# Attention inside a mixture-of-experts layer: query and key weights merged, value weights behind the attention, mask on VectorE

## The reference

```
h = relu(xn @ w1 + b1);  m = h @ w2 + b2
q, k, v = m @ q_w + q_b,  m @ k_w + k_b,  m @ v_w + v_b
# each token attends to the tokens at distance up to 32 of its own sequence
a = softmax(q . k_band / sqrt(128)) @ v_band
# 16 experts, 8 chosen for each token by sigmoid(xn @ gate_w) + expert_bias; weights sum to 2.826
f = sum_e combine[e] * (silu(xn @ w_gate[e]) * (xn @ w_up[e])) @ w_down[e]  +  shared expert
out = x + a + f
```

## Time and profile before

| | |
|---|---|
| median of 3 runs | 744.89 us |
| profiled execution | 746.74 us |
| its span (first to last instruction) | 744.9 us, mean granted TensorE clock 0.997 |
| TensorE matmul | busy 727.2 us, 3544 instructions |
| VectorE | busy 557.6 us, 1344 instructions |
| ScalarE | busy 454.6 us, 904 instructions |
| GpSimd | busy 356.6 us, 294 instructions |

### The profile page before, as it was taken

How to read it: one execution, slowest core, us unless ns; L and a number is a source line. 1 busy time by engine, 2 the same in 40 slices (tenths; PEclk the granted TensorE clock), 3 DMA queues, 4 the chain that set the end, 5 groups by cost and what they waited for, 6 DMA issues and landing times.

```text
span 744.9 us, 10576 instructions
## 1 busy us (share of the span) xinstructions
PE 727.2 (98%) x3544; PEld 593.2 (80%) x3544; DVE 557.6 (75%) x1344; ACT 454.6 (61%) x904; POOL 356.6 (48%) x294
## 2 busy tenths in 40 slices
PE   4899999999999999999999999999999999999997
PEld 3678888888888888888888888888888888888885
DVE  6687777877777787777877777787787877777675
ACT  4685665756566575665756556575655756657473
POOL 3644454544545444454544545444454544545443
PEclk9999999999999999999999999999999999999999
DMA  6605133051520505134051420505124051420500
GB/s 240 256 0 228 44 142 129 3 225 43 201 70 30 227 14 228 43 127 145 2 227 43 176 96 33 212 26 227 44 118 153 1 228 44 178 79 23 220 0 15
DMA packets 23702, 84.59 MB, mean 114 GB/s; under 512 B 2272, under 2 KB 10464, under 8 KB 15456
## 3 DMA queue, kind: packets, MB, share of 16 engines
q1 hardware_dynamic: 23648, 83.91, 29.8%
HBM read 79.19 MB, written 4.72 MB: 113 GB/s over the span
## 4 chain that ended last, share of the span: by engine, by line
PE 94%; DVE 2%; ACT 2%; POOL 1%; DMA 1%; issue 0%; SPq 0%
PE ps_y L362 26%; PE ps_u L352 25%; PE ps_g L342 25%; PE bank L282 6%; PE ps_y L327 3%; PE bank L310 3%; PE bank L287 2%; PE bank L319 2%; PE bank L294 2%; PE bank L300 1%; POOL exp_w_lo L851 1%; PE bank L311 1%; DMA att_raw<-watt 1%; DVE ps_u L817 0%; ACT h_hi L541 0%
## 5 line engine op out<-in xcount | busy, mean ns | idle before, releaser
L891 POOL TENSOR_TENSOR silu_c<-silu,comb_b 128x512 f32<-128x512 f32 x256 | 330.2, 1293 | 369.9 <-ACT silu L533 369.0
L541 ACT ACTIVATE h_hi<-ps_u 128x512 fp32r<-128x512 f32 x272 | 162.5, 598 | 272.5 <-DVE ps_u L817 272.5
L817 DVE TENSOR_TENSOR ps_u<-silu_c,ps_u 128x512 f32<-128x512 f32 x256 | 177.2, 692 | 100.1 <-PE ps_u L352 95.7
L823 DVE TENSOR_TENSOR h_lo<-ps_u,h_hi 128x512 fp32r<-128x512 f32 x272 | 186.8, 687 | 67.3 <-ACT h_hi L541 64.6
L533 ACT ACTIVATE silu<-ps_g 128x512 f32<-128x512 f32 x272 | 161.6, 595 | 0.2
L362 PE MATMUL ps_y<-h_hi,exp_w_hi 128*128 128x512 f32 x272 | 115.2, 424 | 1.1 <-DVE h_lo L823 1.0
L352 PE MATMUL ps_u<-xn_hi,exp_w_hi 128*128 128x512 f32 x272 | 112.2, 412 | 0.9 <-DVE h_lo L823 0.8
L342 PE MATMUL ps_g<-xn_hi,exp_w_hi 128*128 128x512 f32 x272 | 109.6, 403 | 0.3 <-ACT silu L533 0.3
L342 PE MATMUL ps_g<-xn_hi,exp_w_lo 128*128 128x512 f32 x272 | 108.2, 398 | 0.0
L352 PE MATMUL ps_u<-xn_hi,exp_w_lo 128*128 128x512 f32 x272 | 108.1, 397 | 0.0
L352 PE MATMUL ps_u<-xn_lo,exp_w_hi 128*128 128x512 f32 x272 | 107.7, 396 | 0.0
(11 more groups left out here) (113 smaller groups left out, 977.3 us busy)
## 6 DMA issues: line engine op xcount, KB each, us to landing
comb_b<-c_dram SPq DMA_DIRECT2D x64, 1024.0 KB, 6.5
xin<-x SPq DMA_DIRECT2D x16, 256.0 KB, 3.1
xres<-x_t SPq DMA_DIRECT2D x16, 256.0 KB, 2.6
out_t<-xres SPq DMA_DIRECT2D x16, 256.0 KB, 2.0
exp_raw<-wexp SPq DMA_DIRECT2D x3, 960.0 KB, 9.7
c_dram<-comb_t SPq DMA_DIRECT2D x16, 32.0 KB, 1.6
exp_raw<-wexp SPq DMA_DIRECT2D x1, 384.0 KB, 5.7
att_raw<-watt SPq DMA_DIRECT2D x1, 330.5 KB, 4.5
```

The costliest lines, as they stand in the source:

```text
L541: A(h_t[hbuf(par, s)][0][:], ps_u[(par + s) % 2][:], ACT.Copy).then_inc(s_h_hi, 1)
L817: V.tensor_tensor(ps_u[i][:], src[:], ps_u[i][:], ALU.mult).then_inc(s_h, 1)
L823: V.tensor_tensor(t[1][:], ps_u[(par + s) % 2][:], t[0][:].bitcast(F32), ALU.subtract)\
L891: G.tensor_tensor(silu_c[i][:], silu[i][:], comb_b[:, s1 - 1, :], ALU.mult).then_inc(s_silu_c, 1)
```

## The change

1. Scores are q . k = h A h' with A made of q_w, k_w and nm_w2 on both sides, so q_proj applies A to hid_t and the keys are hid_t itself. The bias of the query side that multiplies keys is a vector on q (vecs column 7). The terms that depend on the query alone drop out of the softmax; the kernel makes one such term (key_term, from the transposed hid, key_row and a constant) and uses it in the maximum that the exponent subtracts. k_proj, k_hi and k_lo are gone.
2. hid is transposed (hid_turn, slot 16) and split (hid_n_hi, slot 0; hid_n_lo, slot 1); attend multiplies the weights with it, into bank2, its first product of each sequence 256 columns wide over a zeroed strip so that the whole half bank is started. ScalarE and VectorE split the result (z_hi slot 15, z_lo slot 16), and value_proj multiplies it by the value weights into ps_y, late in slot 0 of the next group. The value projection of slot 7, the transposes of slot 10 and their splits are gone.
3. The mask is fp32, and VectorE adds it in row_max, which takes a tensor_tensor_reduce for each of two tiles (out: the masked scores in SBUF, accumulator: their maximum) and two operations of two columns; exp reads SBUF.
4. scores(0) moves from late to early in slot 3, ahead of down(0).
5. The prologue makes A by a chain of three products of 128 columns with copies between, and the bias vectors; a transfer of 128 KB (watt_t, the transposed q_w and k_w) is added after the first expert weights. The routing of the first group stands behind three one-column copies.

The diff, cut to its core (the renaming of semaphores and tiles and the small steps of VectorE's prologue left out):

```diff
             def scores(seq):
                 ...
                     for n, (a, b) in enumerate(PAIRS3):
-                        mm(o, q_t[a][:, q0:q0 + P], k_t[b][:, k0:k0 + WIN], start=n == 0, stop=False)
-                    done = mm(o, ident_b[:], mask[:, t, :], start=False, stop=True)
+                        done = mm(dst[:, t * SEQ:t * SEQ + WIN], q_t[a][:, q0:q0 + P], hid_t[b][:, k0:k0 + WIN],
+                                  start=n == 0, stop=n == 2)
             def attend(seq):
                 for kb in range(2):
                     col = seq * SEQ + kb * (P - HALF)
-                    for a, b in PAIRS3:
-                        done = mm(ps_y[:, col:col + WIN], v_nat[a][:, seq * 2 + kb, :],
-                                  p_t[b][:, seq, kb, :], start=False, stop=False, skip_group_check=True)
+                    for n, (a, b) in enumerate(PAIRS3):
+                        wide = SEQ if kb == 0 and n == 0 else WIN
+                        done = mm(bank[2][:, col:col + wide], hid_n[a][:, seq * 2 + kb, :],
+                                  p_t[b][:, seq, kb, 0:wide], start=kb == 0 and n == 0, stop=kb == 1 and n == 2,
+                                  skip_group_check=True)
+            def value_proj(g):
+                pe.wait_ge(S["z_lo"], g + 1)
+                for a, b in PAIRS3:
+                    mm(ps_y[:], att_w[a][:, 2, :], z_t[b][:], start=False, stop=False, skip_group_check=True)
             def hid_proj(g, par):
-                if not first(g):
-                    pe.wait_ge(S["v_lo"], g)
+                pe.wait_ge(S["gate_s"], g + 1)
-            def k_proj(g):
+            def hid_turn(g):
                 pe.wait_ge(S["hid_lo"], g + 1)
-                project(bank[0], 2, hid_t).then_inc(S["k_mm"], 1)
+                turn(bank[0], hid).then_inc(S["hid_tp"], 1)
             # TensorE, prologue
-                mm(bank[2][:, 0:3 * P], att_raw[:, W2T:W2T + P], att_raw[:, QKV:QKV + 3 * P],
-                   start=True, stop=True)
+                mm(bank[2][:, M_V:M_V + P], w2t, att_raw[:, QKV + 2 * P:QKV + 3 * P], start=True, stop=True)
                 ...
+                pe.wait_ge(s_wt_in, 16)
+                mm(ps_y[:, M_A:M_A + P], att_t[:, KT:KT + P], att_t[:, QT:QT + P], start=True, stop=True)\
+                    .then_inc(s_qk_mm, 1)
                 ...
                 gate(0)
+                pe.wait_ge(s_qk, 1)
+                pe.wait_ge(s_vec1, 1)
                 pe.wait_ge(s_attw, 1)
+                mm(bank[2][:, M_B:M_B + P], chain[:, 0, :], w2t, start=True, stop=True)
+                mm(bank[2][:, M_VEC + 4:M_VEC + 5], att_t[:, KT:KT + P], vecs[:, 0:1], start=True, stop=True)
+                mm(bank[2][:, M_VEC + 5:M_VEC + 6], att_t[:, QT:QT + P], vecs[:, 1:2], start=True, stop=True)
+                mm(bank[2][:, M_VEC + 6:M_VEC + 7], vecs[:, 0:1].to_broadcast([P, P]), vecs[:, 1:2],
+                   start=True, stop=True).then_inc(s_side_mm, 1)
                 hid_proj(0, 0)
+                pe.wait_ge(s_side, 1)
+                pe.wait_ge(s_vec2, 1)
+                mm(ps_y[:, M_A:M_A + P], w2t, chain[:, 1, :], start=True, stop=True)
+                mm(ps_y[:, M_VEC + 7:M_VEC + 8], w2t, vecs[:, 4:5], start=True, stop=True)
+                mm(ps_y[:, M_B:M_B + P], vecs[:, 5:6].to_broadcast([P, P]), w2t, start=True, stop=True)\
+                    .then_inc(s_score_mm, 1)
                 pe.wait_ge(S["comb"], 1)
-                comb_turn(bank[2])
+                comb_turn(bank[1])
+                pe.wait_ge(s_scw, 1)
+                pe.wait_ge(s_row, 1)
                 q_proj(0)
-                k_proj(0)
+                hid_turn(0)
             # TensorE, att_early
+                if s == 3:
+                    if not first(g):
+                        pe.wait_ge(S["z_lo"], g)
+                    pe.wait_ge(S["q_lo"], g + 1)
+                    scores(0)
                 if s == 4 and more:
                     pe.wait_ge(S["xn_lo"], g + 2)
+                    pe.wait_ge(S["hn_lo"], g + 1)
+                    pe.wait_ge(S["key_term"], g + 1)
                     gate(1 - par)
                 if s == 5:
                     scores(1)
-                if s == 7:
-                    if more:
-                        pe.wait_ge(S["gate_s"], g + 2)
-                    project(bank[0], 3, hid_t).then_inc(S["v_mm"], 1)
-                if s == 10:
-                    pe.wait_ge(S["v_t"], g + 1)
-                    turn(bank[0], v_t).then_inc(S["v_tp"], 1)
             # TensorE, att_late
-                if s == 3:
-                    ...
-                    scores(0)
+                if s == 0 and not first(g):
+                    value_proj(g - 1)
             # TensorE, finish
+                value_proj(GROUPS - 1)
             # ScalarE, prologue
                 xn_hi(0, 0)
+                act.wait_ge(s_qk_mm, 1)
+                A(chain[:, 0, :], ps_y[:, M_A:M_A + P], ACT.Copy, scale=SCALE).then_inc(s_qk, 1)
                 for s in range(0, 2):
                     expw_hi(s)
                 gate_exp(0)
+                act.wait_ge(s_side_mm, 1)
+                A(chain[:, 1, :], bank[2][:, M_B:M_B + P], ACT.Copy).then_inc(s_side, 1)
                 hid_relu(0)
-                for s in range(2, 6):
+                act.wait_ge(s_score_mm, 1)
+                A(att_w[0][:, 1, :], ps_y[:, M_A:M_A + P], ACT.Copy).then_inc(s_scw_hi, 1)
+                A(key_row[:], ps_y[:, M_B:M_B + P], ACT.Copy).then_inc(s_row, 1)
+                for s in range(2, 5):
                     expw_hi(s)
                 comb_out(0, 0)
+                expw_hi(5)
                 q_hi(0)
             # VectorE
+            def hid_n_lo(g):
+                dve.wait_ge(S["hn_hi"], g + 1)
+                V.tensor_tensor(flat(hid_n[1]), bank[0][:], flat(hid_n[0]).bitcast(F32), ALU.subtract)\
+                    .then_inc(S["hn_lo"], 1)
+                ...
+                for a in range(TILES):
+                    done = V.tensor_tensor_reduce(
+                        out=key_prod[:, a, :], in0=bank[0][:, a * P:(a + 1) * P], in1=key_row[:], scale=1.0,
+                        scalar=vecs[:, 6:7], op0=ALU.mult, op1=ALU.add, accum_out=key_term[:, a:a + 1])
+                done.then_inc(S["key_term"], 1)
             def row_max(g, seq):
                 dve.wait_ge(S[f"sc{seq}"], g + 1)
-                V.tensor_reduce(neg_max[:, 2 * seq:2 * seq + 2], halves(score_bank[seq]), AX.X, ALU.max,
-                                negate=True).then_inc(S[f"nmax{seq}"], 1)
+                ...
+                for t in range(2):
+                    done = V.tensor_tensor_reduce(
+                        out=prob[:, 2 * seq + t, :], in0=score_bank[seq][:, t * SEQ:t * SEQ + WIN],
+                        in1=mask[:, t, :], scale=1.0, scalar=TAKEN, op0=ALU.add, op1=ALU.max,
+                        accum_out=score_max[:, 2 * seq + t:2 * seq + t + 1])
+                done.then_inc(S[f"smax{seq}"], 1)
+                dve.wait_ge(S[f"smax{seq}"], g + 1)
+                dve.wait_ge(S["key_term"], g + 1)
+                V.tensor_tensor(full_max[:, n], score_max[:, n], key_term[:, n], ALU.add)\
+                    .then_inc(S[f"fmax{seq}"], 1)
+                dve.wait_ge(S[f"fmax{seq}"], g + 1)
+                V.tensor_tensor(neg_max[:, n], key_term[:, n], full_max[:, n], ALU.subtract)\
+                    .then_inc(S[f"nmax{seq}"], 1)
             # VectorE, att
                 if s == 1:
-                    low_half("k", bank[0], k_t, 1, g)
+                    hid_n_lo(g)
-                if s == 11:
-                    dve.wait_ge(S["v_hi"], g + 1)
-                    V.tensor_tensor(flat(v_nat[1]), bank[0][:], flat(v_nat[0]).bitcast(F32), ALU.subtract)\
-                        .then_inc(S["v_lo"], 1)
-                if s == 16 and more:
-                    low_half("q", bank[1], q_t, 0, g + 1)
+                if s == 16:
+                    z_lo(g)
+                    if more:
+                        q_lo(g + 1)
```

More of the change, by code:

```diff
@@ L84, in layer @@
         ident = sb("ident", [P, P])
-        ident_b = sb("ident_b", [P, P], BF16)
-        mask = sb("mask", [P, 2, WIN], BF16)
+        mask = sb("mask", [P, 2, WIN])
         power = sb("power", [P, TILES])
@@ L102, in layer @@
         q_t = [sb("q_hi", [P, T], F32R), sb("q_lo", [P, T], F32R)]
-        k_t = [sb("k_hi", [P, T], F32R), sb("k_lo", [P, T], F32R)]
-        v_t = sb("v_t", [P, T])
-        v_nat = [sb("v_hi", [P, TILES, P], F32R), sb("v_lo", [P, TILES, P], F32R)]
+        hid_n = [sb("hid_n_hi", [P, TILES, P], F32R), sb("hid_n_lo", [P, TILES, P], F32R)]
+        z_t = [sb("z_hi", [P, T], F32R), sb("z_lo", [P, T], F32R)]
+        key_prod = sb("key_prod", [P, TILES, P])
+        key_term = sb("key_term", [P, TILES])
+        score_max = sb("score_max", [P, TILES])
+        full_max = sb("full_max", [P, TILES])
         neg_max = sb("neg_max", [P, TILES])
@@ L172, in layer @@
```

(46 more changed lines are left out.)

110 lines of the change are left out of this document (68 added, 42 removed).

## The result

| | before | after |
|---|---|---|
| median (range), four runs each | 744.65 us (744.32 to 745.0) | 737.85 us (737.78 to 738.01) |
| ratio after : before, 95% interval | | 0.991 [0.9898, 0.9921] |
| profiled execution's span | 744.9 us | 735.9 us |

The change saves 6.8 us. The direction was forecast and the time lies in the range, but the forecast was a saving of 14.6 us: 7.8 of it did not come.

A forecast was written before the change was run, and what follows sets the result against it. TensorE, 98% busy, was taken as the bound, time being the sum of matmul intervals. Terms -10.5 - 0.7 - 6.1 + 0.3 - 3.9 + 4.8 + 1.5 = -14.6 us gave a 730.3 us median, range 724.5 to 740.5.

The forecast's parts named there:

- What is late next: Slots 5 to 11: up(11) waits for h_lo(9), giving back 0.3 us 16 times, +4.8 us; bounds 0 and twice that.
- ScalarE: less work, none of it on a path: ScalarE loses k_hi, v_t and v_hi, gains hid_n_hi and z_hi; no cost was counted.
- The key projection: Three k_proj matmuls leave TensorE's slot 16, 0.70 us a group, 15 times: -10.5 us.
- the mask: Mask matmuls leave TensorE's scores: 0.19 us a sequence, 32 times, -6.1 us.
- the wide product: First product of attend, 256 columns wide on TensorE: 0.01 us each, 32 times, +0.3 us, at most 1.4.
- scores(0): Slot 3: scores moved ahead of down(0) cover its 0.26 us wait for VectorE, 15 times: -3.9 us.
- c: Time of one 128-column key reduction on VectorE in slot 1: 0.30 us; cover for down(0) thin, ending past 0.35.
- The rival in which VectorE becomes the bound: Key reductions in slot 1 and row_max in slot 6 make the kernel slower; 759 us at 0.70 a reduction; chance 0.10.
- the partial VectorE stall: VectorE reductions of 0.38 to 0.56 us, or operations slowed beside GpSimd, give 734 to 743 us; chance 0.18.
- d: VectorE's row_max, two mask reductions and two tiny operations: 1.1 us; in slot 6 cost zero up to 1.4.
- The prologue, +1.5: Before the main loop: weight chain, copies, later GpSimd and key reductions cost +1.5 us, between -0.5 and +4.
- value_proj in the tail: Last group: three value matmuls lie in TensorE's 1.00 us idle time before the last down projection: -0.7 us once.

The follow-up runs named there:

- e8: Kernel after with one move: the next group's hid_proj goes from slot 13 to slot 7; 729.08 us.
- e5: Kernel before with only scores(0) of slot 3 put ahead of down(0); 741.66 us.
- e10: e9 with the mask put back on TensorE, one bf16 matmul a tile, and a plain negated maximum on VectorE; 731.73 us.
- e9: Kernel after with the changes of e7 and e8 together, and without the prologue products and copies that only feed the key term; 724.99 us.
- e2: Kernel after with the two maxima and their sum kept in PSUM, so each tiny operation has one SBUF input; 737.06 us.
- e4: Kernel after with the mask back on TensorE, one plain negated maximum over 320 columns, no key reductions, exps reading PSUM; 736.05 us.
- e7: Kernel after without key reductions and tiny operations: negative scores, minimum straight into neg_max, masked scores kept in PSUM for the exps; 732.51 us.
- e1: Kernel after without the four key reductions of slot 1, key_term being a column of zeros; 736.39 us.
- e3: Kernel after with row_max writing masked scores back to their PSUM bank, where the exps read them; 736.15 us.

## Why the prediction was wrong in its size

**"What is late next" failed.** It went the right way, asked what the shorter TensorE work would run into, named ScalarE's silu of 403.40 with its two table loads and four exps, and then followed that chain on to its end (VectorE, h_lo(9), up(11)) rather than asking at each link who on TensorE needs it and with what slack. The first need is gate_proj(9), 0.66 us behind; 0.89 us were being taken from ahead of it. "ScalarE: less work, none of it on a path" was right on the sum (8.1 us less busy) and wrong on the path: the work that left stood elsewhere, and the exps that stayed, which are on the path, became slower (0.41 us for 0.37). The stall is 44.08 - 43.51 = 0.57 us a group in place of 0.3, and 14 groups at 0.27 make 3.8 us. (The steady state is off by less, 3.0 over 13 groups, since the other terms together were 0.04 a group too low.) The bound "twice that" held the size, but for the wrong cause.

**The key projection, the mask, the wide product, scores(0): right in sum.** The period of e8 has their sum, 1.32 us, to within 0.02 to 0.04. One by one, scores(0) measured 0.28 to 0.30 for 0.26 (e5) and the mask 0.46 for 0.38 (e10 against e9); the key projection and the wide product were not measured alone. The Trainium skill (TensorE: Matmul & The Clock Gate, "Back-to-back issue gap") would have priced the three matmuls of the key projection at 0.39 us, an estimate by which the sum is 1.01; the period fell by 1.34 to 1.36, so for this fp32r stream the row decides.

**c: on the high side.** Two of the key reductions of the kernel after, VectorE's timeline:

```profile
340.28 0.34 DVE L757 CUSTOM_DVE_ANT_0 key_prod<-bank,key_row,vecs 128x128 f32<-128x128 f32 x1
340.55 0.09 DVE L757 DVE_READ_ACCUMULATOR2_ANT key_term<- 128x1 f32 x1
340.55 0.35 DVE L757 CUSTOM_DVE_ANT_0 key_prod<-bank,key_row,vecs 128x128 f32<-128x128 f32 x1
```

0.27 us from one to the next, for 0.30 taken. (The prediction's steps add up to 435.4 + 4c and not 435.5 + 4c, and the cover then ends at c = 0.40 and not 0.35; at 0.27 neither matters.) As the Trainium skill says (VectorE: DVE Perf Modes, "Two Vector instructions with no wait between them"), the accumulator is an instruction of its own: the row of 0.09 us. But the next reduction starts at the same 340.55, so it adds nothing visible. The rival in which VectorE becomes the bound needed c = 0.56 and is out, and so is the partial VectorE stall as it was described, though 737.85 lies among its times (734 to 743): a reader who goes by the time alone would take it for right.

**d: 1.35 us for 1.1, for a reason that wasn't in the sum.** VectorE's timeline of the kernel after, slot 6:

```profile
351.42 0.32 DVE L821 CUSTOM_DVE_ANT_0 prob<-bank,mask 128x160 f32<-128x160 f32 x1
...
352.02 0.63 DVE L828 TENSOR_TENSOR full_max<-score_max,key_term 128x2 f32<-128x2 f32 x1
352.69 0.16 DVE L831 TENSOR_TENSOR neg_max<-key_term,full_max 128x2 f32<-128x2 f32 x1
352.77 0.69 DVE L905 TENSOR_TENSOR ps_u<-silu_c,ps_u 128x512 f32<-128x512 f32 x1
```

From 351.42 to 352.77. "Free up to 1.4" held where the prediction looked: h_prod(5) ends at 353.46, and ScalarE comes to h_hi(5) at 353.57. Behind it VectorE's row makes h_lo(5) and with it up(7) late, which costs the period nothing (e2).

**The first group had no term.** VectorE there still makes the low halves of expert weights, and the new work queues behind them. VectorE's timeline of the kernel after, first group, and TensorE's wait that follows:

```profile
35.34 1.02 DVE L663 TENSOR_TENSOR exp_w_lo<-exp_raw,exp_w_hi 128x384 fp32r<-128x384 f32 x1
36.29 0.31 DVE L821 CUSTOM_DVE_ANT_0 prob<-bank,mask 128x160 f32<-128x160 f32 x1
...
36.88 1.12 DVE L828 TENSOR_TENSOR full_max<-score_max,key_term 128x2 f32<-128x2 f32 x1
...
38.12 0.68 DVE L911 TENSOR_TENSOR h_lo<-ps_u,h_hi 128x512 fp32r<-128x512 f32 x1
38.72 0.69 DVE L905 TENSOR_TENSOR ps_u<-silu_c,ps_u 128x512 f32<-128x512 f32 x1
```

```profile
45.43 0.50 PE L381 MATMUL ps_u<-xn_hi,exp_w_hi 128*128 128x512 f32 x1 [1.77 <-DVE h_lo L911]
```

row_max lasts 38.12 - 36.29 = 1.83 us, h_prod(4) starts at 38.72, and with it ScalarE's gapless row and up(7) are late. The period grew by 1.36 where a fall of 1.02 was forecast. e4, without this row_max, has 46.35, and e7, without the tiny operations, has 46.25, so it accounts for the growth of 1.3 us. The fall that is still missing is in part the same hole: e8 has 46.91, 0.70 less than the kernel after, and e9, with both, 45.61 where the forecast was 45.23. The last 0.4 us are open.

**The prologue, +1.5: mis-sized within its bounds.** +3.36 us up to the first scores(1), where the prediction's terms give 1.3. Two of its waits in TensorE's timeline of the kernel after:

```profile
27.31 0.66 PE L307 MATMUL bank<-ident,xn 128*128 128x128 f32 x4 [1.55 <-DVE xn L683]
30.66 0.50 PE L381 MATMUL ps_u<-xn_hi,exp_w_hi 128*128 128x512 f32 x1 [1.30 <-DVE h_lo L911]
```

Before, undisturbed, the first is at 24.26, so 3.05 us are lost by then. GpSimd, whose low halves end later, comes to rstd at 24.07 for 22.05, which is 2.0 of them, and the four normalisations that wait for it last 2.13 us for 1.11, which is the other 1.0. The second is the key sums' place (e1: -1.18). How the 2.0 divide among the longer chain and its copies was not taken apart; leaving the key term out of the chain (e9) brings the first scores(1) only to 35.87.

**The zero of the sum: no part of the miss.** The forecast subtracted from a profiled execution with a low-clock stretch at 26 to 30 us and treated its distance of 1.85 us to the median as a constant. The kernel after, at clock 0.999, is 9.0 us below that span and 6.8 below by the medians. The forecast for the median keeps its 14.6 either way; its 0.42 us a matmul in the prologue was read from that stretch, and in the kernel after the same gate matmuls are 0.23 apart (28.51, 28.74, 28.97).

**value_proj in the tail: right.** The tail of the kernel after (it answers to the earlier trace rows):

```profile
728.91 0.50 PE L358 MATMUL ps_y<-z_hi,att_w_hi 128*128 128x512 f32 x1
...
731.63 0.50 PE L391 MATMUL ps_y<-h_hi,exp_w_hi 128*128 128x512 f32 x1 [0.37 <-DVE h_lo L911]
```

The idle time before the last down is 0.37 us in place of 1.00, for 0.70 of work moved into it.

## What to carry to other kernels

When work is taken off the engine that sets the time, find in every other engine the longest row without idle time, and for each of its results the slack on the engine that needs it; work taken from ahead of that need is worth no more than the slack, wherever the engine's total stands. If the slack is short, move other work of the bounding engine into the hole: here three matmuls moved six slots gave more (8.8 us) than the whole change had (6.8). And look in new algebra for terms that cancel: the key term cost 1.5 us here in its sums alone (e1) and does not change the exponent.

## What was not expected of the hardware

A VectorE operation of two columns on two SBUF inputs lasts 0.16 us alone, 0.63 in slot 6 and up to 1.12 (mean 426 ns, 32 times), and 168 ns on average with one input in PSUM (e2). In the two places shown above, where it is long, it ends with GpSimd's product of 512 columns. GpSimd's timeline of the kernel after, first group and mid-run:

```profile
36.69 1.30 POOL L977 TENSOR_TENSOR silu_c<-silu,comb_b 128x512 f32<-128x512 f32 x1 [0.74 <-ACT silu L580]
```

```profile
351.35 1.29 POOL L977 TENSOR_TENSOR silu_c<-silu,comb_b 128x512 f32<-128x512 f32 x1 [1.56 <-ACT silu L580]
```

These end at 37.99 and 352.64, the long VectorE operations (36.88 + 1.12 and 352.02 + 0.63) at 38.00 and 352.65. That the one waits for the other is inferred from these ends and from e2. The Trainium skill (GPSIMD Engine Reference, "Specifications") says that GpSimd's SBUF interfaces are shared with VectorE, with contention for VectorE instructions with two SBUF inputs, and this case agrees.

An exp of 160 columns with its accumulator starts 0.41 us before the next when it reads SBUF and 0.37 when it reads PSUM (e3). After each of the three late starts above, TensorE's second matmul comes 0.34 us after the first in place of 0.233 (0.31 behind transposes): the stop in the running stream, at up(7), cost 0.1 us more than its idle time.
